# A graph-attention kernel whose last quarter of byte transposes moves from TensorE to a transposing DMA

## What is computed

```python
h = jnp.maximum(_layernorm(x, axis=-1), 0.0)
Wh = h @ W
a1, a2 = (a[:Fout, 0], a[Fout:, 0])
e = (Wh @ a1)[:, None] + (Wh @ a2)[None, :]
e = jnp.where(e > 0, e, ALPHA * e)
e = jnp.where(adj > 0, e, MASK_VAL)
attention = jax.nn.softmax(e, axis=1)
x = x + jax.nn.elu(attention @ Wh)
```

## Time and profile before

| what | us |
|---|---|
| three runs | 246.78, 248.80, 249.32 |
| profiled execution | 247.97 |
| its span | 246.2 |
| TensorE busy (matmul) | 227.2 |
| VectorE busy | 196.3 |
| ScalarE busy | 169.8 |
| HBM read, written | 69.27 MB, 2.10 MB |

### The profile page before, as it was taken

How to read it: one execution, slowest core, us unless ns; L and a number is a source line. 1 busy time by engine, 2 the same in 40 slices (tenths; PEclk the granted TensorE clock), 3 DMA queues, 4 the chain that set the end, 5 groups by cost and what they waited for, 6 DMA issues and landing times.

```text
span 246.2 us, 8267 instructions
## 1 busy us (share of the span) xinstructions
PE 227.2 (92%) x3736; PEld 221.2 (90%) x3736; DVE 196.3 (80%) x259; ACT 169.8 (69%) x149; POOL 59.0 (24%) x48
## 2 busy tenths in 40 slices
PE   6958999599999999999999999999999999999770
PEld 2748899599999999999999999999999999999770
DVE  4997988437776898889888988898889888988935
ACT  3699975696799999994996679219976795020051
POOL 3647027798000070300000560000003700040000
PEclk9997999999999999999999999999999999999996
DMA  6999999999999999999999999999999200020002
GB/s 216 352 387 387 385 388 386 386 319 337 304 333 325 335 388 386 386 385 385 397 387 386 388 386 388 386 386 376 385 387 384 89 3 0 3 88 3 0 3 91
DMA packets 36521, 71.92 MB, mean 292 GB/s; under 512 B 1282, under 2 KB 1924, under 8 KB 36484
## 3 DMA queue, kind: packets, MB, share of 16 engines
q1 hardware_dynamic: 35520, 69.74, 78.6%
q10 hardware_dynamic: 964, 1.64, 1.8%
HBM read 69.27 MB, written 2.10 MB: 290 GB/s over the span
## 4 chain that ended last, share of the span: by engine, by line
PE 77%; DVE 10%; issue 4%; POOL 4%; ACT 2%; DMA 1%; DVEq 0%; POOLq 0%
PE acc L834 21%; PE acc L835 21%; PE acc L836 21%; PE mask_t L817 11%; DVE words L610 3%; POOL v L330 2%; POOL val L333 2%; DVE stats L547 1%; DMA x_sb<-in_x_dram 1%; PE acc L805 1%; ACT v L508 1%; PE acc L796 1%; DVE wh_sb L573 1%; PE mask_t L785 1%; DVE hp L718 1%
## 5 line engine op out<-in xcount | busy, mean ns | idle before, releaser
L610 DVE SCALAR_TENSOR_TENSOR words<-g_row,gq_word,mask_t 128x1024 f32<-128x1024 f32 x128 | 161.1, 1277 | 36.7 <-PE acc L836 18.8
L834 PE MATMUL acc<-val,words 128*128 128x129 f16 x992 | 170.6, 220 | 1.2 <-DVE num L618 0.9
L835 PE MATMUL acc<-val,words 128*128 128x129 f16 x992 | 170.6, 220 | 0.0
L836 PE MATMUL acc<-val,words 128*128 128x129 f16 x992 | 170.6, 220 | 0.0
L420 ACT ACTIVATE mask<-raw,step_bias 128x2048 uint8<-128x2048 int32 x63 | 121.7, 1993 | 21.9 <-DVE x_sb L626 13.5
L834 PEld LDWEIGHTS acc<-val,words 128*128 128x128 f16 x992 | 97.1, 98 | 1.5 <-DVE words L610 1.0
L835 PEld LDWEIGHTS acc<-val,words 128*128 128x128 f16 x992 | 97.1, 98 | 0.1
L836 PEld LDWEIGHTS acc<-val,words 128*128 128x128 f16 x992 | 97.1, 98 | 0.0
L817 PE MATMUL mask_t<-ident_b,mask 128*128 128x128 bf16 x512 | 34.7, 222 | 1.4 <-ACT mask L420 1.4
L817 PEld LDWEIGHTS mask_t<-ident_b,mask 128*128 128x128 bf16 x512 | 30.8, 100 | 1.6 <-ACT mask L420 1.5
L358 POOL TENSOR_TENSOR hp<-num,rz 128x1024 f32<-128x1024 f32 x3 | 5.7, 1898 | 106.3 <-DVE rz L621 106.3
(11 more groups left out here) (94 smaller groups left out, 147.1 us busy)
## 6 DMA issues: line engine op xcount, KB each, us to landing
raw<-in_adj_dram SPq DMA_DIRECT2D x64, 1024.0 KB, 13.8
x_sb<-in_x_dram SPq DMA_DIRECT2D x8, 256.0 KB, 5.7
out_dram<-x_sb ACTq DMA_DIRECT2D x3, 512.0 KB, 7.5
out_dram<-x_sb SPq DMA_DIRECT2D x2, 128.0 KB, 1.9
out_dram<-x_sb SPq DMA_DIRECT2D x1, 192.0 KB, 2.0
w_sb<-in_L_gnn_W_dram ACTq DMA_DIRECT2D x1, 64.0 KB
out_dram<-x_sb SPq DMA_DIRECT2D x1, 64.0 KB, 1.7
a_sb<-in_L_gnn_a_dram ACTq DMA_DIRECT2D x1, 1.0 KB
```

The costliest lines, as they stand in the source:

```text
L610: nc.vector.scalar_tensor_tensor(words[:, q], g_row[:, c * CHUNK:(c + 1) * CHUNK], gq_word[:, 1, t:t + 1], maskt_bytes[:, u % 2, q // 2, : ...
L834: nc.tensor.matmul(acc_tile(t), high, val[:, tile, 0, 0:V], start=first and t % PT == 0, stop=False, skip_group_check=True)
L835: nc.tensor.matmul(acc_tile(t), high, val[:, tile, 1, 0:V], start=False, stop=False, skip_group_check=True)
L836: last = nc.tensor.matmul(acc_tile(t), low, val[:, tile, 0, 0:V], start=False, stop=False, skip_group_check=True)
```

## The change

1. The rows of the graph are numbered anew: row = 256d + 2p + e, d being a pair of tiles. In return, a load of half a unit is two DMAs of 512 KB and not one of 1 MB (pieces of 2 KB in both), an `x` load or a store has pieces of 1 KB and not 2 KB, and the last result is stored by three DMAs and not four.
2. The two bytes of a pair are now bytes whose bf16 elements lie next to each other for one transpose (`mask_pairs` is `(h j)` and not `(j h)`).
3. For chunk 3, TensorE's transposes are gone. Behind the bytes of each of its units, ScalarE issues one transposing DMA (`turn_beside`), 512 KB from the `mask` slot to an SBUF buffer: `h_t` for blocks 0 and 1, `v32` for 2 and 3, the first two tiles of a `raw` slot for 4 to 7. Before the issue, ScalarE waits for its own bytes (`act_bytes`) and for the words of chunk 1.
4. VectorE's words of chunk 3 read the bytes from SBUF and wait for the DMA (`beside[u]`) and not for `turned`; ScalarE's bytes of units 28 to 31 wait for the DMA that has read the slot.

The diff, without the parts for the general path, which is not executed on these inputs:

```diff
--- before.py
+++ after.py
@@ -46,6 +46,7 @@
     G = NB // 2
     C = N // CHUNK
     U = NB
+    BESIDE = (C - 1) * U
     V = F + 1
     W2 = F + 2
     VP = 160
@@ -53,12 +54,13 @@
     BANKS = ((0, 3), (3, 6), (6, 8))
     assert F == P and w.shape == (F, F) and N == 4096
 
-    x_v = x.rearrange("(b p q) f -> b p q f", p=P, q=BT)
-    out_v = out.rearrange("(c b p q) f -> c p b q f", b=2, p=P, q=BT)
-    adj_v = adj.rearrange("(c b p q) (u j) -> c b u p q j", b=2, p=P, q=BT, j=BLOCK)
-
+    x_v = x.rearrange("(b g p e) f -> b p g (e f)", g=2, p=P, e=2)
+    out_v = out.rearrange("(c d p e) f -> c p d (e f)", d=4, p=P, e=2)
+    adj_v = adj.rearrange("(c d p e) (u j) -> c d u p e j", d=4, p=P, e=2, j=BLOCK)
+
 
     with ExitStack() as ctx:
         def sb(name, shape, dt):
@@ -134,9 +136,14 @@
 
         words_h = words[:].bitcast(F16).rearrange("p s (i e) -> p s i e", e=2)
         gq_word_h = gq_word[:].bitcast(F16).rearrange("p u (t e) -> p u t e", e=2)
-        mask_pairs = mask[:].bitcast(BF16).rearrange("p s t (j h) -> p s t j h", h=2)
+        mask_pairs = mask[:].bitcast(BF16).rearrange("p s t (h j) -> p s t h j", h=2)
         maskt_pairs = mask_t[:].bitcast(BF16)
         maskt_bytes = mask_t[:].bitcast(U8).rearrange("p s h (i e) -> p s h i e", e=2)
+
+
+        beside_bufs = [h_t[:, 0:2], h_t[:, 2:4], v32[:, 0], v32[:, 1]] + [raw[:, s, 0:2] for s in range(RING)]
+        beside_pairs = [s.rearrange("p a b -> p (a b)").bitcast(BF16).rearrange("p (m i) -> p m i", i=P) for s in beside_bufs]
+        beside_bytes = [s.rearrange("p a b -> p (a b)").bitcast(U8).rearrange("p (t h i e) -> p t h i e", h=2, i=P, e=2) for s in beside_bufs]
 
         def acc_tile(t):
             return acc[:, t // PT, (t % PT) * V:(t % PT + 1) * V]
@@ -160,6 +167,7 @@
         first_bytes = sem("first_bytes")
         act_bytes = sem("act_bytes")
         turned = sem("turned")
+        beside = [sem(f"beside{u}") for u in range(U)]
         words_ready = sem("words_ready")
         words_free = sem("words_free")
         acc_done = sem("acc_done")
@@ -229,7 +237,7 @@
         gen_res = sem("gen_res")
         gen_out = sem("gen_out")
         GEN_STEPS = 10
-        OUT_DMAS = C - 1 + 4
+        OUT_DMAS = C - 1 + 3
 
         block = ctx.enter_context(nc.Block())
 
@@ -243,10 +251,11 @@
         @block.sync
         def _(sp):
             def load_x(b):
-                sp.dma_start(x_sb[:, b * BT:(b + 1) * BT, :], x_v[b]).then_inc(x_in[b], 16)
+                sp.dma_start(x_sb[:, b * BT:(b + 1) * BT, :].rearrange("p (g e) f -> p g (e f)", e=2), x_v[b]).then_inc(x_in[b], 16)
 
             def load_raw(n, k):
-                sp.dma_start(raw[:, n % RING, k * BT:(k + 1) * BT], adj_v[n // U, k, n % U]).then_inc(raw_in[n % RING][k], 16)
+                for d in (2 * k, 2 * k + 1):
+                    sp.dma_start(raw[:, n % RING, 2 * d:2 * d + 2], adj_v[n // U, d, n % U]).then_inc(raw_in[n % RING][k], 16)
 
             for b in range(4):
                 load_x(b)
@@ -265,31 +274,33 @@
                         sp.wait_ge(act_bytes, 2 * (n - RING) + k)
                     load_raw(n, k)
 
-            last = x_sb[:, (C - 1) * CT:C * CT]
+            def store_last(d0, d1):
+                sp.dma_start(out_v[C - 1, :, d0:d1], x_sb[:, (C - 1) * CT + 2 * d0:(C - 1) * CT + 2 * d1].rearrange("p (d e) f -> p d (e f)", e=2)
+                             ).then_inc(out_done, 16)
+
             sp.wait_ge(last_res, 1)
-            sp.dma_start(out_v[C - 1, :, 0, 0:3], last[:, 0:3]).then_inc(out_done, 16)
+            store_last(0, 1)
             sp.wait_ge(last_res, 2)
-            sp.dma_start(out_v[C - 1, :, 0, 3:4], last[:, 3:4]).then_inc(out_done, 16)
-            sp.dma_start(out_v[C - 1, :, 1, 0:2], last[:, 4:6]).then_inc(out_done, 16)
+            store_last(1, 3)
             sp.wait_ge(last_res, 3)
-            sp.dma_start(out_v[C - 1, :, 1, 2:4], last[:, 6:8]).then_inc(out_done, 16)
+            store_last(3, 4)
 
...
             sp.wait_ge(out_done, 16 * OUT_DMAS)
@@ -413,12 +424,22 @@
 
             def to_bytes(c, u, k):
                 n = c * U + u
-                act.wait_ge(raw_in[u % RING][k], (2 * c + u // RING + 1) * 16)
-                if n >= RING:
-
+                act.wait_ge(raw_in[u % RING][k], (2 * c + u // RING + 1) * 32)
+
+                if n >= BESIDE + RING:
+                    act.wait_ge(beside[u - RING], 16)
+                elif n >= RING:
                     act.wait_ge(turned, n - RING + 1)
                 nc.scalar.activation(mask[:, u % RING, k * BT:(k + 1) * BT], raw[:, u % RING, k * BT:(k + 1) * BT], ACT.Sigmoid,
                                      scale=64.0, bias=step_bias[:, 0:1]).then_inc(act_bytes, 1)
+
+            def turn_beside(u):
+
+                act.wait_ge(act_bytes, 2 * (BESIDE + u) + 1)
+
+                act.wait_ge(words_ready, BT * (BESIDE - U))
+                act.dma_start(beside_pairs[u], mask_pairs[:, u % RING].rearrange("p t h j -> p (t h j)"), transpose=True
+                              ).then_inc(beside[u], 16)
 
             def row_copy(g, k):
                 act.wait_ge(spread_ps, 2 * g + k + 1)
@@ -485,17 +506,20 @@
 
             def store(c):
                 act.wait_ge(res_ready, c + 1)
-                act.dma_start(out_v[c].rearrange("p b q f -> p b (q f)"),
-                              x_sb[:, group(c)].rearrange("p (b q) f -> p b (q f)", b=2)).then_inc(out_done, 16)
+                act.dma_start(out_v[c], x_sb[:, group(c)].rearrange("p (d e) f -> p d (e f)", e=2)).then_inc(out_done, 16)
 
             for c in range(1, C):
                 for u in range(6):
                     for k in range(2):
                         to_bytes(c, u, k)
+                    if c == C - 1:
+                        turn_beside(u)
                 tail(c - 1)
                 for u in range(6, U):
                     for k in range(2):
                         to_bytes(c, u, k)
+                    if c == C - 1:
+                        turn_beside(u)
                 store(c - 1)
 
             nc.scalar.activation(warm[:], warm[:], ACT.Exp).then_inc(warm_ready, 1)
@@ -601,14 +625,21 @@
             def weights(c, u, q):
                 n = c * U + u
                 if q % 2 == 0:
-                    if q == 0:
+                    if q == 0 and n < BESIDE:
                         dve.wait_ge(turned, n + 1)
                 if n >= 1:
 
                     dve.wait_ge(words_free, 4 * n + q - WORDS + 1)
                 t = u * BT + q
-                nc.vector.scalar_tensor_tensor(words[:, q], g_row[:, c * CHUNK:(c + 1) * CHUNK], gq_word[:, 1, t:t + 1],
-                                               maskt_bytes[:, u % 2, q // 2, :, q % 2], ALU.max, ALU.mult).then_inc(words_ready, 1)
+                word, row = words[:, q], g_row[:, c * CHUNK:(c + 1) * CHUNK]
+                if n < BESIDE:
+                    turned_bytes = maskt_bytes[:, u % 2, q // 2, :, q % 2]
+                else:
+                    if q == 0:
+                        dve.wait_ge(beside[u], 16)
+                    turned_bytes = beside_bytes[u][:, :, q // 2, :, q % 2]
+                    word, row = (v.rearrange("p (t i) -> p t i", i=P) for v in (word, row))
+                nc.vector.scalar_tensor_tensor(word, row, gq_word[:, 1, t:t + 1], turned_bytes, ALU.max, ALU.mult).then_inc(words_ready, 1)
 
             def take_sums(c):
 
@@ -814,7 +845,7 @@
                     pe.wait_ge(words_ready, 4 * (n - 1))
                 for h in range(2):
                     for t in range(CT):
-                        last = nc.tensor.transpose(maskt_pairs[:, u % 2, h, t * P:(t + 1) * P], mask_pairs[:, u % RING, t, :, h], ident_b[:])
+                        last = nc.tensor.transpose(maskt_pairs[:, u % 2, h, t * P:(t + 1) * P], mask_pairs[:, u % RING, t, h], ident_b[:])
                 last.then_inc(turned, 1)
 
             def product(c, u, q):
@@ -924,7 +955,8 @@
                     if (c, u) == (C - 1, U - 1):
                         last_product()
                     else:
-                        turn(c, u + 1)
+                        if c * U + u + 1 < BESIDE:
+                            turn(c, u + 1)
                         for q in range(BT):
                             product(c, u, q)
```

More of the change, by code:

```diff
@@ L54, in bass_graph_attention @@
     assert F == P and w.shape == (F, F) and N == 4096
[L56 to L61 removed]
+    x_v = x.rearrange("(b g p e) f -> b p g (e f)", g=2, p=P, e=2)
+    out_v = out.rearrange("(c d p e) f -> c p d (e f)", d=4, p=P, e=2)
+    adj_v = adj.rearrange("(c d p e) (u j) -> c d u p e j", d=4, p=P, e=2, j=BLOCK)
+    x_rows_v = x.rearrange("(d p e) f -> d p e f", p=P, e=2)
+    adj_rows_v = adj.rearrange("(d p e) j -> d p e j", p=P, e=2)
+    out_rows_v = out.rearrange("(d p e) f -> d p e f", p=P, e=2)
     with ExitStack() as ctx:
```

24 lines of the change are left out of this document (11 added, 13 removed).

## The result

| what | before | after |
|---|---|---|
| median of five runs, us | 248.2 | 259.9 |
| lowest, highest | 246.78, 249.32 | 259.02, 266.06 |
| span of the profiled execution | 246.2 | 261.4 |

The change makes the kernel slower: ratio 1.0456, 95% interval 1.0414 to 1.0498. Executions more than 1.5% above the fastest of their kernel count as slow and stay out of every ratio, here 263.27 (the profiled one) and 266.06; the other three have a median of 259.03 us. The profiled execution is 3.4 us above the median of all five.

A forecast was written before the change was run, and what follows sets the result against it. The prediction took TensorE to bound the kernel; -7.1 for transposes, +0.6 handoff and -0.4 end gave -6.9 us, so 241.1 or 241.9 us by baseline, taken as 241.5. The range was 240.0 to 251 us, leaving out the slow rival.

The forecast's parts named there:

- What bounds the kernel, and what is removed: TensorE in chunk 3, 6.33 us per unit; eight units' transposes at 0.89 us each go, 7.1 us off.
- T, issue to landing: Time from issue to landing of one 512 KB transpose: 5.2 us in the mean, hidden up to 6.5.
- H, ScalarE's hold: How long issuing one transpose holds ScalarE: about 1 to 2 us, free up to 2.5, gain gone at 3.4.
- 200.9 + 8H: When the last transpose is out of ScalarE, in us, set against 221.2, when word (31, 0) wants it.
- VectorE, 42.8 us of 43.5: VectorE's work in chunk 3, 42.8 us, fits within TensorE's 43.5 us with 0.7 us to spare.
- the case: Rival in which VectorE becomes the bound, SBUF reads beside DMA lengthening words: 243 to 244 us, chance 5%.
- Handoff: Between chunks 2 and 3, TensorE newly waits for a bank's sum: 0.6 us added, bounds 0.4 to 0.9.
- End: Last store goes out earlier with one store fewer ahead of it: 0.4 us off, bounds 0 and 0.6.
- Start: Loads of `x` in 1 KB pieces at the start: nothing taken, bounds 0 and +0.5 us.
- Sums: Range's low edge put at 240.0 us from handoff 0.4, end -0.6, the run's own time; DMA full until about 185 us.
- the second: Rival: transposes slower than a plain DMA pace chunk 3, 257 us at T = 8.5, 260 at H = 4.9; chance 20%.

The follow-up runs named there:

- the copy: The changed kernel with each of the eight transposing DMAs made a plain copy of the same 512 KB to the same buffer: 244.07 us, ratio 0.9855.
- the quiet kernel: The changed kernel without the loads of units 28 to 31, whose bytes are made from what the slots hold: 244.46 us, ratio 0.9874.
- the last experiment on GpSimd: The changed kernel with all its loads, GpSimd's tail of chunk 2 working on one of eight row tiles: median 262.89 us.

## Why the prediction was wrong

- **What bounds the kernel, and what is removed**: right as far as the words keep up. The pitch is 6.33 us per unit with TensorE's transposes, and with only the last four units changed, each gives back its 0.89 us in full. With all eight, even where no transpose came late, VectorE was the bound (below).
- **T, issue to landing**: this step failed. It took the landing of plain stores, 7.5 us beside loads and 2.9 alone, and their mean, 5.2. A transposing DMA of the same bytes took 10.4 to 17.3 us beside the loads and 4.3 to 4.6 behind them. The bounds went wrong before the mean did: the slowest store beside the loads, 8.5 us, was taken for the worst case. The copy has the stores' prices; the transposing DMA has its own, and what it takes from the loads comes on top: 264 GB/s in place of 385. The sentence "the loads end by 190 us" treated the loads as given. The last one landed at 194.3 us even before, and at 214.5 in the changed kernel, 20 us later (1.7 of them from the late start).
- **H, ScalarE's hold**: this step failed too. 1 to 2 us is what was measured behind the loads in this kernel (up to 3.1 in others); beside loads it was 4.9 to 11.2, in the mean 4.5 over all eight. The prediction's own sum, 200.9 + 8H, gives 237.1 us for the end of the last hold (it was 239.65, in an execution that began 1.7 later), and 241.5 + 237.1 - 221.2 = 257.4 us for the kernel. The formula also has a gap: word (31, 0) is not ready when the last hold ends but when that transpose lands, 2.3 us later (241.9 us). With that, the free H shrinks from 2.5 to about 2.25 us, and the sum gives 259.7. The chain that ended last runs through ScalarE's holds (13% of the span) where it was to run through TensorE. H and T were priced as two separate risks; here both went up together, where loads ran beside the transposes. I read that as the queue holding its issuer while the engines are behind, which no run tests by itself.
- **VectorE, 42.8 us of 43.5**: the case was named, but its source wasn't. The pitch of words from SBUF is 1.20 to 1.27 us, as taken. But the stretch was 3.7 to 4.1 us longer than 42.8 where no DMA was late, and the rows put all of that beside GpSimd's operations: words whose bytes come from SBUF and GpSimd's tail hold each other up. In the changed kernel this shows as 2.0 us. By the sum, it is what keeps the quiet kernel and the copy, 244.5 and 244.1, from 241; taking it away gave that in two runs of ten. The Trainium skill has the rule in "SBUF — State Buffer", section "Who interferes with whom": a VectorE instruction with two inputs in SBUF contends with a GpSimd instruction that reads SBUF. This trace agrees: L369 2.77 us beside such words, 1.90 beside words from PSUM.
- **Handoff**: right, 0.7 us of wait on `num` against 0.6. **End**: right in size, about 0.3 us against 0.4. **Start**: right as far as it can be told; the renumbering alone measures 0.6 us (0 to 1.3), taken was nothing, with a bound of 0.5. **Sums**: with a handoff of 0.4, an end of -0.6 and the run's own time, the low edge of the range comes to 240.7 and not 240.0, which changes nothing here; the engines were full to 191 us and not 185.
- **The rivals**: the second, transposes slower than a plain DMA that pace chunk 3, happened, at 257 to 260 us as worked out. That the time fits is in part luck: its T of 8.5 us and H of 4.9 are bounds from plain transfers, and the first four measured well above T and up to 11.2 us of H, the last four well below both. It had 20%, because its reason against was that the loads end by 190 us, with nothing said of what the transposes do to the loads.
- **The Trainium skill's two rules on the transposing DMA** both fall short. "DMA: Bandwidth & Descriptors", section "Latency and other measured facts", with 261 GB/s, gave an estimated 2.0 us for 512 KB; alone it is 4.3, about 120 GB/s with the latency in it. The 32 cycles a tile of "Why a DMA increments its semaphore by 16 and not by 1" gave an estimated hold of 3.4 us; alone it is mostly 1.7 to 2.0 and up to 3.1, and beside loads up to 11.2.

## What to carry to other kernels

Cost a transposing DMA in time of the DMA engines, not in bytes: find its price alone, and do not take a plain transfer's price for it. Ask what it takes from the loads of the same stretch, since in these runs both were served by the same engines, the loads ended 20 us later, and whoever issued the transposes was held longer while loads ran beside them. Put such transfers where the loads are over, and only as many as fit there; the four that fitted gave their whole gain. When a hold sits in an engine's program, remember that the last transfer still has to land behind the last hold. And when an operand moves from PSUM to SBUF, look at what GpSimd does in that stretch.

## What the runs showed of the hardware

- A transposing DMA of 512 KB from SBUF to SBUF, 16-bit elements: 4.2 to 5.7 us from issue to landing with no loads beside it, in most cases under 4.8, and 1.7 to 2.0 us of hold of its issuer, in a few cases 2.8 to 3.1. In the changed kernel, beside raw loads: 10.4 to 17.3 us and 4.9 to 11.2 us. The plain copy: 2.9 us and 0.47 us alone, up to 8.1 and 0.53 beside loads.
- With these transposes, the DMA engines read as fully busy (1.10) at 264 GB/s, and with copies in their place (1.04) at 385; a share near 1 says that they have work, not how many bytes flow.
- A GpSimd add of 128x1024, 2.37 us otherwise, took 10.22 us while VectorE made words with two inputs in SBUF back to back, and single words of VectorE took 2.9 to 3.4 us in place of 1.28 while GpSimd worked. Which of the two yields differs from place to place; what decides it stays open.
- Executions with the same program at the start reach their first product at 27.34 to 29.98 us (the quiet kernel's profile and that of the last experiment on GpSimd). The difference arises at two places: in the 16 projections at 9 us (2.23 or 2.79 to 2.87 us) and in those at 23 us (2.00 to 3.26 us). The second comes behind 3.4 us in which TensorE idles; its granted clock in 20 to 30 us was between 0.72 and 1.00 in the profiles of this study.
